# Unread products, one moved gate product and a GpSimd broadcast in a four-layer decoder

## The chip, the cores and the metric

The kernel runs on one core of one Trainium2 chip. The metric is the device time of one execution in microseconds (us); a comparison takes the median of several executions. Besides those, one execution was taken with the hardware profiler, and all rows below come from it.

## The reference

Eight sequences of 56 tokens with 256 channels go through four decoder layers in 32-bit floats. Each layer has three blocks with a residual and a LayerNorm behind each:

```
x = _layernorm(x + attention(x))        # self-attention, another kind in each layer
x = _layernorm(x + cross(x, ctx_512))   # attention over a context of 1500 positions of 64 channels
x = _layernorm(x + experts(x))          # router, top-k, gated experts and a shared expert
```

In layers 0, 2 and 3 the cross-attention has 16 heads, folds the key weights into the query, takes a softmax over the 1500 positions, and multiplies the weights with the rotated context. In layer 1 it attends, under a causal mask, over the first 56 positions of the context. The feed-forward blocks compute `silu(x @ gate) * (x @ up)`, weight it with the router's top-k scores, and multiply with `down`. Only the final `x` is written.

## The kernel before, in words

The program is one sequence of twelve stages (three for each layer). Each stage gives every engine its own list of instructions; nothing schedules them, the order is the one in which the code is written, and engines wait for one another by semaphores with constants (`wait_ge`). A stage's `begin` waits for the normalised `x_feat` (features by tokens) that the stage before put into SBUF. Weights come by DMA from SyncE, mostly a stage ahead.

A TensorE product in 32-bit floats shows as two matmul rows in the trace, one for each pass; the listings of the program's order show it as one. The eight PSUM banks are shared out by number.

- `keep_busy(c, bank, n, rhs, cols)` (L164 to L170) issues `n` products of 128 by `cols` into a bank that nothing reads. It stands at many places in the kernel, each ahead of a wait or between short instructions.
- `cross_attention` (L767 and on, layers 0, 2 and 3). For a pair of sequences, 16 heads by 56 tokens make seven blocks of 128 rows, so four pairs make 28 blocks ("i"), each holding both sequences of its pair. Block i goes through `score` (six products of 500 columns, L1035), maxima on VectorE (L1315, L1320), `exp` on ScalarE (L1236), division on VectorE (L1328), `turn` (48 transposes of 64 columns on TensorE, L1122, in three groups of 16), copies out of PSUM (VectorE L1334 for one group, ScalarE L1243 for two), `weigh` (L1135) and a small copy on GpSimd (L908). The loop at the end of the TensorE list does, for each i, `score(i)`, `weigh(i-2)`, `turn(i-1)`. In its first pass (i = 1) there is no `weigh`, and two `keep_busy` calls stand there. The second group of turnings waits for the exponential of block 1's first half, and the third for that of its second half, since they reuse those banks.
- `feed_forward` (L1429 and on, all layers). TensorE first multiplies `x` with the router (L1483), then for chunk after chunk of 128 hidden columns with `gate` and `up` (`gate_up`, L1501: two products each). VectorE makes the top-k weights from the router's logits; TensorE turns them (`widen`, L1516), VectorE copies them (`wide_out`, L1712), GpSimd spreads one row over all partitions for each chunk (L1474, `partition_broadcast`), VectorE multiplies (L1637), and TensorE does the second product of the chunk (`down`, L361).
- `SmallHeads.tensor` (L1809 and on; layer 1's self- and cross-attention and layer 2's self-attention). Between the scores of the first and of the second group of heads, TensorE waits for VectorE to empty the banks (L1914), with a `keep_busy` ahead of the wait: two products where there is no mask, which is layer 1's self-attention alone.
- `l3_attention` (L2490 and on). Low-rank updates are folded into the weights: TensorE makes the update (`lora`, L2556, L2560), VectorE adds it to the weight (L2720). After the first two updates stands a `keep_busy` of 256 columns, then the first full round of updates, then the values (L1965).

## Time and profile before

| | us |
|---|---|
| three executions | 1661.98, 1663.19, 1670.23 (median 1663.19) |
| the profiled execution, its own time | 1660.22 |
| its span, first to last instruction | 1658.4 |
| TensorE busy in the span | 1620.9 (98%) |
| VectorE / ScalarE / GpSimd busy | 1114.3 / 750.3 / 240.8 |

The span is what the rows below lie in; 1.8 us lie outside it. The granted clock of TensorE is given as a share of 2.4 GHz: 1.00 is that, 0.50 is 1.2 GHz. Its mean over the span is 0.997.

### The profile page before, as it was taken

To read this page: it belongs to the slowest core of one execution; us is meant where nothing else is said; L and a number is where in the kernel's file an instruction comes from. 1 tells how busy PE (TensorE), PEld (TensorE's weight loads), DVE (VectorE), ACT (ScalarE), POOL (GpSimd) and SP (SyncE) were. 2 spreads that over 40 slices of the span, in tenths; PEclk is the share of its full clock that TensorE was granted. 3 is DMA by queue.
4 is the path that set the end of the run, shared out by engine and by line. 5 is a ranking of instruction groups with operands and counts; after the bars stand their busy time and mean duration, and the time that the engine had idled before them with its cause. 6 is when DMAs were issued, how large, how long until landed. Compare 5 with 4: busy or idle time off the path is not lost.

```text
span 1658.4 us, 35648 instructions
## 1 busy us (share of the span) xinstructions
PE 1620.9 (98%) x15234; PEld 1100.1 (66%) x15234; DVE 1114.3 (67%) x1974; ACT 750.3 (45%) x1297; POOL 240.8 (15%) x431
## 2 busy tenths in 40 slices
PE   9999999999999999999999999999999999999998
PEld 5575367777755666655377777764566767777765
DVE  2725889999566763266899999535445289999633
ACT  2223366666412641143366666312454366666411
POOL 0011300000011312011200000010465000000030
PEclk9999999999999999999999999999999999999999
DMA  9312020000040011051020000060300220000010
GB/s 281 84 16 83 1 78 2 2 2 2 2 188 1 2 59 40 1 127 55 1 97 2 2 2 2 2 243 0 64 1 1 115 90 2 2 2 2 2 45 11
DMA packets 35523, 71.10 MB, mean 43 GB/s; under 512 B 25359, under 2 KB 29776, under 8 KB 31434
## 3 DMA queue, kind: packets, MB, share of 16 engines
q1 hardware_dynamic: 35240, 68.71, 12.7%
q8 instruction: 121, 1.98, 0.5%
q14 instruction: 36, 0.29, 0.1%
q10 hardware_dynamic: 126, 0.11, 0.0%
HBM read 68.36 MB, written 0.46 MB: 41 GB/s over the span
## 4 chain that ended last, share of the span: by engine, by line
PE 90%; DVE 6%; ACT 2%; issue 1%; DMA 1%; POOL 0%; DVEq 0%; ACTq 0%; POOLq 0%
PE ps L1122 14%; PE ps L1135 14%; PE ps L1035 13%; PE ps L361 9%; PE ps L1501 9%; PE ps L946 3%; PE ps L2603 3%; PE ps L1150 3%; PE ps L528 2%; PE ps L1965 2%; PE ps L956 1%; PE ps L2630 1%; PE ps L982 1%; PE ps L967 1%; PE ps L523 1%
## 5 line engine op out<-in xcount | busy, mean ns | idle before, releaser
L1236 ACT ACTIVATE arena<-ps,softmax_stats 128x1500 f32<-128x1500 f32 x168 | 254.0, 1512 | 194.0 <-DVE softmax_stats L1317 192.0
L1135 PEld LDWEIGHTS ps<-arena,ctx_pos 125*64 125x64 f32 x4608 | 222.3, 137 | 58.4 <-issue 56.1
L1122 PE MATMUL ps<-ident,arena 64*125 64x64 f32 x4032 | 239.5, 271 | 1.9 <-ACT arena L1236 1.6
L1135 PE MATMUL ps<-arena,ctx_pos 125*64 125x128 f32 (+1 forms) x4608 | 240.5, 262 | 0.0
L1122 PEld LDWEIGHTS ps<-ident,arena 64*125 64x125 f32 x4032 | 227.1, 186 | 17.0 <-issue 13.5
L1035 PE MATMUL ps<-ctx_feat,arena 64*128 64x500 f32 x1008 | 231.7, 592 | 0.0
L1243 ACT COPY arena<-ps 125x512 f32<-125x512 f32 x336 | 172.5, 599 | 78.2 <-PE ps L1122 78.2
L1315 DVE TENSOR_REDUCE softmax_stats<-ps 128x1 f32<-128x500 f32 x252 | 170.7, 679 | 50.4 <-PE ps L1035 50.1
L361 PE MATMUL ps<-arena 128*128 128x256 f32 x736 | 174.9, 384 | 4.9 <-DVE arena L1630 1.2
L1328 DVE TENSOR_SCALAR arena<-arena,softmax_stats 128x1500 f32<-128x1500 f32 x168 | 168.3, 1002 | 5.9
L1501 PE MATMUL ps<-x_feat,arena 128*128 128x448 f32 (+1 forms) x416 | 164.6, 540 | 1.2 <-DVE arena L1613 1.2
L361 PEld LDWEIGHTS ps<-arena 128*128 128x128 f32 x736 | 136.9, 190 | 43.0 <-issue 16.6
L908 POOL COPY arena<-arena 64x128 f32<-64x128 f32 (+1 forms) x186 | 51.5, 277 | 683.7 <-DVE arena L1341 677.6
L1320 DVE TENSOR_REDUCE softmax_stats<-ps 128x1 f32<-128x1500 f32 x84 | 143.6, 1709 | 0.0
L1035 PEld LDWEIGHTS ps<-ctx_feat,arena 64*128 64x128 f32 x1008 | 90.0, 189 | 80.5 <-issue 77.9
L1501 PEld LDWEIGHTS ps<-x_feat,arena 128*128 128x128 f32 (+1 forms) x416 | 78.0, 190 | 63.6 <-issue 59.6
L1334 DVE COPY arena<-ps 125x512 f32<-125x512 f32 x168 | 107.6, 682 | 12.8 <-PE ps L1122 12.5
L1577 ACT ACTIVATE arena<-ps 128x448 f32<-128x448 f32 (+1 forms) x52 | 28.3, 544 | 188.3 <-PE ps L1501 183.9
L1613 DVE TENSOR_TENSOR arena<-ps,arena 128x448 f32<-128x448 f32 x41 | 25.6, 624 | 113.7 <-ACT arena L1577 86.0
L946 PE MATMUL ps<-x_feat,arena 128*128 128x448 f32 x128 | 56.1, 563 | 0.2
L2603 PE MATMUL ps<-x_feat,arena 128*128 128x448 f32 x128 | 52.4, 552 | 1.2 <-issue 0.7
L2731 DVE TENSOR_TENSOR arena<-ps,arena 128x448 f32<-128x448 f32 x32 | 20.0, 625 | 46.0 <-ACT arena L2675 45.9
(325 smaller groups left out, 1923.7 us busy)
## 6 DMA issues: line engine op xcount, KB each, us to landing
ctx_pos<-in_ctx SPq DMA_DIRECT2D x1, 2688.0 KB
arena<-in_L1f_gate SPq DMA_DIRECT2D x1, 2304.0 KB, 11.9
arena<-in_L1f_up SPq DMA_DIRECT2D x1, 2304.0 KB, 16.9
arena<-in_L1f_down SPq DMA_DIRECT2D x1, 2304.0 KB, 7.7
arena<-in_L0a_Wq SPq DMA_DIRECT2D x1, 2048.0 KB, 10.9
arena<-in_L0a_Wc SPq DMA_DIRECT2D x1, 2048.0 KB, 18.8
arena<-in_L0x_Wq SPq DMA_DIRECT2D x1, 2048.0 KB, 10.1
arena<-in_L0x_Wo SPq DMA_DIRECT2D x1, 2048.0 KB, 8.5
```

The source lines that it names most:

```text
L361: m = c.nc.tensor.matmul(y_of(c, s, j), lhsT, rhs, start=False, stop=last, skip_group_check=True)
L946: m = nc.tensor.matmul(c.ps[:, 2 + h % 2, 0:NT], wq[:, k, h, :], c.x_feat[:, k, :, 0:T], start=(k == 0), stop=(k == KT - 1))
L1035: m = nc.tensor.matmul(sc[e][:, k, :], q[e * 64:(e + 1) * 64], c.ctx_feat[e * 64:(e + 1) * 64, j, k * 4 * LP:(k + 1) * 4 * LP], start=True ...
L1122: m = nc.tensor.transpose(c.ps[0:LP, turn_bank(i, k, r), n * 64:(n + 1) * 64], probs[i % 2][e][rows, l * LP:(l + 1) * LP], c.ident[rows, r ...
L1135: m = nc.tensor.matmul(y[r * 64:(r + 1) * 64, lo:hi], c.ctx_pos[:, j, l, e, :], pT[i % 2][:, lo // 64:hi // 64, LT * e + l, :], start=(l = ...
L1236: nc.scalar.activation(probs[i % 2][e].rearrange("p (k l) -> p k l", k=3), sc[e], ACT.Exp, bias=low[:, i % 4, e:e + 1], accum_out=total[:, ...
L1243: nc.scalar.copy(pT[i % 2][:, r, 8 * k:8 * k + 8, :], c.ps[0:LP, turn_bank(i, k, r), :].rearrange("p (s q) -> p s q", s=8)).then_inc(*a_in ...
L1315: nc.vector.tensor_reduce(peak[:, i % 4, k:k + 1], sc[0][:, k, :], AX.X, ALU.max).then_inc(*maxed.next())
L1320: nc.vector.tensor_reduce(low[:, i % 4, 1:2], sc[1], AX.XY, ALU.max, negate=True).then_inc(*lowered[1].next())
L1328: nc.vector.tensor_scalar(probs[i % 2][e], probs[i % 2][e], inv[:, i % 4, e:e + 1], None, ALU.mult).then_inc(*normed[e].next())
L1334: nc.vector.tensor_copy(pT[i % 2][:, r, 0:8, :], c.ps[0:LP, turn_bank(i, 0, r), :].rearrange("p (s q) -> p s q", s=8)).then_inc(*d_in.next())
L1501: m = nc.tensor.matmul(c.ps[0:m_, bank(n) + i, 0:NT], w[:, k, n * 128:n * 128 + m_], c.x_feat[:, k, :, 0:T], start=(k == 0), stop=(k == KT ...
```

## The change

1. In `cross_attention`, the `keep_busy` of 512 columns in the pass i = 1 issues two products instead of one (layers 0, 2 and 3).
2. In `SmallHeads.tensor`, the `keep_busy` without a mask issues four products instead of two (layer 1's self-attention).
3. In `l3_attention`, the `keep_busy` behind the first two updates has 512 columns instead of 256.
4. In `feed_forward` of layers 2 and 3, the first of the two gate products of chunk 0 is issued ahead of the router's products instead of behind them.
5. At the end of each `cross_attention`, GpSimd spreads four numbers of the identity matrix over all partitions into a new tile `reach`, which nothing reads, and waits until that is done.

```diff
@@ cross_attention, gpsimd @@
         pool.wait_ge(ct_in.handle, ct_in.last())
+        nc.gpsimd.partition_broadcast(c.reach[:], c.ident[0:1, 0:4], channels=128).then_inc(*warmed.next())
+        pool.wait_ge(warmed.handle, warmed.last())
@@ cross_attention, tensor, loop over i @@
                 pe.wait_ge(cm_act.handle, cm_act.at(3))
-                keep_busy(c, 6, 1)
+                keep_busy(c, 6, 2)
                 keep_busy(c, 6, 1, None, 256)
@@ feed_forward, tensor @@
         pe.wait_ge(c.loaded[name].handle, 16 * c.expect[name])
+        gate_first = kind in ("L2", "L3")
+
+        def gate_of_first(k):
+            m_ = f.chunks[0][0]
+            nc.tensor.matmul(c.ps[0:m_, bank(0), 0:NT], wg[:, k, 0:m_], c.x_feat[:, k, :, 0:T], start=(k == 0), stop=(k == KT - 1))
+
+        if gate_first:
+            gate_of_first(0)
         for j in range(J):
...
             for i, w in enumerate((wg, wu)):
                 for k in range(KT):
+                    if gate_first and (n, i, k) == (0, 0, 0):
+                        continue
@@ SmallHeads.tensor @@
             if g == 1:
-                keep_busy(c, 6, 2 if self.mask is None else self.waiting)
+                keep_busy(c, 6, 4 if self.mask is None else self.waiting)
@@ l3_attention, tensor @@
-        keep_busy(c, 6, 1, None, 256)
+        keep_busy(c, 6, 1)
```

TensorE in the cross-attention of layer 0, from the last fold of the output weights (L937) over the scores of blocks 0 and 1 to the first turnings, before and then now (line numbers are of each kernel's own file):

```order
L937 MATMUL ps<-arena 64x256 x8
L1035 MATMUL ps<-ctx_feat,arena 128x500 x6
L170 MATMUL ps<-ctx_feat,ident 128x512
L170 MATMUL ps<-ctx_feat,ident 128x256
L1122 MATMUL ps<-ident,arena 125x64 x48
```

```order
L940 MATMUL ps<-arena 64x256 x8
L1038 MATMUL ps<-ctx_feat,arena 128x500 x6
L171 MATMUL ps<-ctx_feat,ident 128x512 x2
L171 MATMUL ps<-ctx_feat,ident 128x256
L1125 MATMUL ps<-ident,arena 125x64 x48
```

One more product of 512 columns stands ahead of the 48 turnings; the same holds in layers 2 and 3.

TensorE at the start of layer 2's feed-forward, from the last filler of the cross-attention to the first `down`; the products of 9 columns are the router, the turnings of 128x128 the widening:

```order
L170 MATMUL ps<-ctx_feat,ident 128x256
L314 MATMUL ps<-ident,x_tok 128x128 x2
L186 MATMUL ps<-x_tok,ident 128x256
L1477 UNCONDITIONAL_BRANCH
L1483 MATMUL ps<-arena,x_feat 128x9 x8
L1501 MATMUL ps<-x_feat,arena 128x448 x8
L1516 MATMUL ps<-ident,arena 128x128 x8
L1501 MATMUL ps<-x_feat,arena 128x448 x4
L361 MATMUL ps<-arena 128x256 x4
```

```order
L171 MATMUL ps<-ctx_feat,ident 128x256
L315 MATMUL ps<-ident,x_tok 128x128 x2
L187 MATMUL ps<-x_tok,ident 128x256
L1480 UNCONDITIONAL_BRANCH
L1488 MATMUL ps<-x_feat,arena 128x448
L1494 MATMUL ps<-arena,x_feat 128x9 x8
L1514 MATMUL ps<-x_feat,arena 128x448 x7
L1529 MATMUL ps<-ident,arena 128x128 x8
L1514 MATMUL ps<-x_feat,arena 128x448 x4
L362 MATMUL ps<-arena 128x256 x4
```

One gate product went ahead of the router, and the seven others of chunks 0 and 1 stayed behind it; the number of products is the same.

GpSimd from the last copies of layer 2's cross-attention to the broadcasts of its feed-forward:

```order
L908 COPY arena<-arena 64x64 x4
L908 COPY arena<-arena 64x128 x4
L1457 UNCONDITIONAL_BRANCH
L1461 MEMSET arena 128x8x8 x2
L1462 MEMSET arena 128x1536
L1463 MEMSET arena 128x4x8
L1474 ISA
L1474 ISA arena<-arena 128x448 x10
```

```order
L909 COPY arena<-arena 64x64 x4
L909 COPY arena<-arena 64x128 x4
L911 ISA
L911 ISA reach<-ident 128x4
L1460 UNCONDITIONAL_BRANCH
L1464 MEMSET arena 128x8x8 x2
L1465 MEMSET arena 128x1536
L1466 MEMSET arena 128x4x8
L1477 ISA arena<-arena 128x448 x10
```

The library change (the `ISA` row without operands) went with the new broadcast from the feed-forward to the end of the cross-attention. Layers 0 and 3 show the same.

## Rows read from the trace of the kernel before

**Rows 1.** The page: each engine's busy us, its share of the span, instructions.

```profile
PE 1620.9 (98%) x15234; PEld 1100.1 (66%) x15234; DVE 1114.3 (67%) x1974; ACT 750.3 (45%) x1297; POOL 240.8 (15%) x431
```

**Rows 2.** Windows: length, each engine's busy us, granted clock, DMA share, GB/s.

```profile
79.00:82.40 3.40, 3.40 (x26) 2.12 (x24) 1.77 (x3) 0.54 (x1) 0.70 (x1) 0.50 1.03 333
215.50:218.90 3.40, 2.77 (x43) 2.42 (x42) 3.32 (x5) 2.80 (x4) 0.00 (x0) 1.00 1.03 431
218.90:222.35 3.45, 3.45 (x20) 1.97 (x18) 2.01 (x4) 2.05 (x4) 0.00 (x0) 0.51 0.97 394
834.06:837.46 3.40, 2.77 (x43) 2.42 (x42) 3.32 (x5) 2.80 (x4) 0.00 (x0) 1.00 0.97 404
837.46:840.91 3.45, 3.45 (x28) 1.53 (x26) 2.79 (x6) 2.05 (x4) 0.00 (x0) 1.00 1.01 427
```

**Rows 3.** Timeline of TensorE: start, us, operation, [idle before, releaser]; layers 0 and 2.

```profile
218.38 1.43 PE L1122 MATMUL ps<-ident,arena 64*125 64x64 f32 x16 [0.54 <-ACT arena L1236]
219.60 4.12 PE L1035 MATMUL ps<-ctx_feat,arena 64*128 64x500 f32 x12
...
834.14 2.26 PE L1122 MATMUL ps<-ident,arena 64*125 64x64 f32 x32
836.94 1.08 PE L1122 MATMUL ps<-ident,arena 64*125 64x64 f32 x16 [0.54 <-ACT arena L1236]
837.86 2.92 PE L1035 MATMUL ps<-ctx_feat,arena 64*128 64x500 f32 x12
...
843.48 2.83 PE L1122 MATMUL ps<-ident,arena 64*125 64x64 f32 x48
```

**Rows 4.** Timeline of VectorE, layer 2's cross-attention, first turnings.

```profile
836.43 1.29 DVE L1334 COPY arena<-ps 125x512 f32<-125x512 f32 x2
837.83 1.00 DVE L1328 TENSOR_SCALAR arena<-arena,softmax_stats 128x1500 f32<-128x1500 f32 x1
840.82 0.68 DVE L1315 TENSOR_REDUCE softmax_stats<-ps 128x1 f32<-128x500 f32 x1 [0.34 <-PE ps L1035]
```

**Rows 5.** The chain that ended last, layer 2's feed-forward: start, us, what.

```profile
1085.01 0.64 DVE arena L1712
...
1085.69 2.05 issue
1087.73 0.75 POOL arena L1474
```

**Rows 6.** Timeline: TensorE's wait in layer 2's feed-forward, and GpSimd around library changes.

```profile
1089.48 1.99 PE L361 MATMUL ps<-arena 128*128 128x256 f32 x8 [1.06 <-DVE arena L1637]
...
1056.25 0.64 POOL L908 COPY arena<-arena 64x128 f32<-64x128 f32 x2 [7.49 <-DVE arena L1341]
1076.48 0.23 POOL L1461 MEMSET arena<- 128x64 f32 x2 [19.58 <-DVE x_feat L265]
1087.73 5.03 POOL L1474 PARTITION_BROADCAST arena<-arena  x7 [9.64 <-issue]
...
1592.78 1.36 POOL L1474 PARTITION_BROADCAST arena<-arena  x2 [8.29 <-DVE arena L1712]
```

**Rows 7.** Timeline of TensorE, layer 1's self-attention, between two groups of scores.

```profile
542.00 1.88 PE L170 MATMUL ps<-ctx_feat,ident 128*128 128x512 f32 x4
545.73 1.12 PE L1827 MATMUL ps<-arena 32*64 32x112 f32 x64 [1.85 <-DVE arena L1914]
```

**Rows 8.** The chain that ended last, start of layer 3's self-attention.

```profile
1135.24 0.63 PE ps L170 x2
1135.88 0.43 PE ps L2556
```

**Rows 9.** Timeline, layer 2's feed-forward: first gate and up products, router's weights, first widening.

```profile
1078.28 6.26 PE L1501 MATMUL ps<-x_feat,arena 128*128 128x448 f32 x16
1083.28 0.22 DVE L1698 TENSOR_TENSOR arena<-arena 128x32 f32<-128x32 f32 x1
1084.37 1.04 PE L1516 MATMUL ps<-ident,arena 128*128 128x128 f32 x8
```

More of the change, by code:

```diff
@@ L69, in __init__ @@
         self.warm = sb("warm", [128, 1])
+        self.reach = sb("reach", [128, 4])
         self.std = sb("std", [128, J])
@@ L820, in cross_attention @@
         s.sem(x) for x in ("maxed", "turned_lo", "turned_hi", "d_in", "a_in", "pv_mm", "kept", "ct_in", "ct_last"))
-    cm_mm, padded = s.sem("cm_mm"), s.sem("padded")
+    cm_mm, padded, warmed = s.sem("cm_mm"), s.sem("padded"), s.sem("warmed")
     cm_act, cm_dve = s.sem("cm_act"), s.sem("cm_dve")
```

## The prediction, written before the changed kernel ran

> **What bounds the kernel now.** I read the page first. TensorE is busy for 1620.9 of 1658.4 us [rows 1], so only 37.5 us of its time are idle, and an edit that takes no product away can win no more than some waits and whatever time TensorE spends at its lower clock. The change takes no product away. I then read the granted clock over the span in windows. It falls to 1.2 GHz in two places: for 3.45 us in layer 0's cross-attention (0.51), and for 3.40 us in layer 0's self-attention (0.50), which the change leaves alone [rows 2]. Last I read the timeline and the chain that ended last at each of the edited places.
>
> **The low clock and the extra filler in the cross-attentions.** Layers 0 and 2 run the same instructions there, so one is the price list of the other. In both, the 3.40 us around the first turnings have TensorE busy for 2.77 us with 43 matmuls. In layer 0 the clock then fell to 0.51; in layer 2 it stayed at 1.00 [rows 2]. The low stretch costs this: from the start of the third group of turnings to the end of the next scores, layer 0 takes 219.60 + 4.12 - 218.38 = 5.34 us and layer 2 takes 837.86 + 2.92 - 836.94 = 3.84 us [rows 3]. TensorE is on the path in both, so a low stretch here is worth 1.50 us.
>
> The Trainium skill (TensorE: Matmul & The Clock Gate, "What's actually happening") says that the gate watches activity on its own beat, which does not restart with the kernel. By it two equal stretches may end differently, and this trace agrees: 2.77 us busy in both, 0.51 behind one and 1.00 behind the other [rows 2]. By that rule an unchanged kernel gets another number of low stretches in each execution; this is the second rival below.
>
> The new product of 512 columns is issued three times (layers 0, 2, 3). Two such products take 1.88 us in layer 1 [rows 7], so one takes 0.94. What covers it is TensorE's own idle time ahead of the third group of turnings, which waits for ScalarE's second exponential (0.54 us in both layers [rows 3]). The least cover is the 0.63 us that TensorE is idle in the stretch (3.40 - 2.77 [rows 2]). The most follows from the unhindered rate of turnings, 48 in 2.83 us: 32 of them need 1.89, and from 834.14 to 836.94 there are 2.80, which leaves 0.91 [rows 3]. So each filler puts 0.03 to 0.31 us on the path. I take 0.10, near the end that comes from back-to-back turnings, since those behind the filler no longer wait for the first exponential: 0.30 us for the three. The second group of turnings gets later by about half a microsecond, and with it VectorE's copies of it (836.43), the division (837.83) and the next block's maxima; VectorE still waits 0.34 us for TensorE before 840.82 [rows 4], and ahead of that for two more scores, so I put nothing on that.
>
> **The broadcast at the end of the cross-attentions.** In layer 2's feed-forward the chain runs through 2.05 us of "issue" on GpSimd between VectorE's copy of the widened weights, which ends at 1085.65, and the first broadcast at 1087.73 [rows 5]. Nothing that the profile shows holds GpSimd there; it has been without a busy instruction for 9.64 us since its memsets [rows 6]. The only thing between them is the library change. In layer 3 there were 8.29 us between, and what released the broadcast was VectorE's copy [rows 6]. So I read the change of library as lasting 8 us or less there, and 9.6 us where layer 3's weights were arriving at the same time. Moved behind the last copy of the cross-attention, which ends at 1056.89, it begins 19.6 us ahead of the next memset at 1076.48 [rows 6]. 9.64 for the library and 0.75 for a broadcast, taken as long as one of 448 columns [rows 5], are 10.4; the new wait holds up only those memsets, and has 9.2 us to spare. Layers 0 and 3 have the same gap. VectorE and TensorE do not wait for this broadcast.
>
> TensorE waited 1.06 us for the first weighted tile [rows 6]. The broadcast can move forward by up to 2.05 us, and then TensorE is last, with the products of the third chunk. The gain is 1.06 us, bounded by 0 (the delay stays) and 2.05 (all of the gap).
>
> The Trainium skill (GPSIMD Engine Reference, "2.1 Instruction dispatch") says that the first call into freshly loaded code costs about 6 us, seen as a gap behind the configuring instruction with no row of its own. The gap without a row agrees, the size does not: 9.64 us here [rows 6]. With 6 us the library would have been ready at about 1084, ahead of the data, and this part would give nothing; the sum below would then come out 1.06 us higher.
>
> **The gate product ahead of the router (layers 2 and 3).** It is moved, not added. A product is two of the 16 rows that take 6.26 us, so 0.78 us [rows 9], and the router's logits come that much later. Behind them VectorE's work on the weights ended at 1083.50, and TensorE began to widen them at 1084.37, when it was through with its products [rows 9]: 0.87 us of slack against 0.78. Bounds are 0 and 0.78 for each layer; I take 0.10 each, since TensorE fetches the weights of a turning a little before it begins: 0.20 us. Neither layer shows a low clock here, so nothing comes back.
>
> **The filler in layer 1's self-attention.** Two more products of 512 columns are 1.88 us, against 1.85 us that TensorE waits for VectorE right behind them [rows 7]. I take 0.05, with bounds 0 and 1.88.
>
> **The filler in layer 3's self-attention.** Here the chain runs through the filler itself: 0.63 us for 256 columns, and the next update right behind it [rows 8]. No wait covers it, so twice the columns cost more: at least 0.94 - 0.63 = 0.31, at most 0.63 again. Half of 0.94 is 0.47, which I take.
>
> **Sum against the profiled execution.** -1.50 (low stretch of layer 0) - 1.06 (broadcast) + 0.30 + 0.20 + 0.05 + 0.47 = -1.54 us. From 1660.22 that is 1658.7. The median of the three runs is 1663.19, which is 2.97 us above the profiled execution: as much as two more low stretches at 1.50. If they lie elsewhere, the change gives 1663.19 - 1.54 = 1661.65; if one of them lies at an edited place and goes too, 1660.15. I say 1661.0, between the two, nearly 0.13% below the median. A measurement of this kernel can tell 0.5% from no change, 8.3 us, so this is "no change" by that bound.
>
> **Rivals.**
> - *The low stretches only move.* If filler does not decide where the clock falls, the median keeps its low stretches and the change is -1.06 + 1.02 = -0.04: 1663.15. For it: the equal stretches with unequal ends [rows 2]. Against it: TensorE's idle time in the stretch that preceded the fall is filled.
> - *The library was not what delayed the broadcast.* Then the 1.06 us stay: 1661.0 + 1.06 = 1662.1. Against it: nothing else stands between the memsets and the broadcast.
> - *The fillers meet a low clock and stand on the path.* TensorE takes its instructions in order, so a filler at 1.2 GHz pushes everything behind it. At half the clock one takes 1.88 us: 3 x (1.88 - 0.63) + (3.76 - 1.85) + 0.94 = 6.6 us, less 1.06 for the broadcast, +5.5: 1668.7, slower than before. It decides as soon as the clock has already fallen when the filler starts. Against it: the clock was at 1.00 when the turnings behind the present filler began, in layer 0 too [rows 2], and the full price needs the fall at every place; one place costs 0.9 to 1.9 us.
>
> **How the numbers follow.** Forecast 0.62, stretches only move 0.20, library not the cause 0.08, fillers on the path 0.10. For the range the low end is 1656.5: the profiled execution with this change is 1658.7, and less the low stretch of layer 0's self-attention, 1.50, is 1657.2, with the rest of the broadcast's bound below that. The high end is 1666.5: half of the third rival's extra, and the three runs of before reach 1670.23, so a median can sit a few us high. For faster by over 0.5% it would have to fall below 1654.9, which no sum of the gains from the fastest execution reaches: 0.03. For slower by over 0.5% it would have to pass 1671.5, above even the third rival: 0.03. That leaves 0.94.
>
> **What would show each step.** In the profile after: GpSimd's first broadcast in layer 2's feed-forward 0.2 to 0.3 us behind the copy of the widened weights, and no wait for VectorE ahead of the first `down` of that stage; the granted clock at 1.00 through the first turnings of all three cross-attentions, with the idle time ahead of the third group at 0.1 or less; layer 1's wait of 1.85 us gone, with the next scores at the same distance from VectorE's subtraction; the update rounds of layer 3 some 0.45 us later against the first two updates; the first widening of layers 2 and 3 at most 0.2 us later against the start of its stage. The prediction is wrong if the wait for the first tile stays, if a low stretch follows the fillers, or if the median leaves 1656.5 to 1666.5.

## The result, and the profile after

The changed kernel took 1656.45 us (median of 8 runs, 1655.58 to 1664.71) against 1664.80 for the kernel before in the same comparison (8 runs, 1661.98 to 1674.96). The ratio is 0.9949, with a 95% interval from 0.9924 to 0.9973: faster by 8.35 us or 0.5%. I had forecast 1661.0 and a range from 1656.5; the time lies 0.05 us below that range. Of the gain I had forecast a quarter (2.2 us below 1663.19), and I had called it "no change". By the prediction's own bound of 0.5% it is just over, with the interval on both sides of that bound; that it is not zero is clear. The profiled execution of after took 1655.68 us, with a span of 1653.9 and a mean granted clock of 0.999.

In the windows of the profile after (columns as in [rows 2]), the first two rows are layer 0's cross-attention around the first turnings, the third layer 2's, the fourth layer 3's, the fifth layer 0's self-attention. They answer to [rows 2]:

```profile
212.00:215.42 3.42, 3.42 (x22) 1.86 (x22) 3.15 (x6) 2.12 (x3) 0.00 (x0) 1.00 0.86 293
215.42:218.84 3.42, 3.42 (x46) 2.64 (x44) 2.88 (x5) 2.25 (x5) 0.00 (x0) 1.00 1.02 427
834.20:837.60 3.40, 3.40 (x26) 1.54 (x26) 3.12 (x7) 2.05 (x4) 0.00 (x0) 1.00 1.01 428
1342.00:1345.40 3.40, 3.40 (x50) 2.66 (x50) 3.11 (x5) 1.79 (x2) 0.00 (x0) 1.00 0.88 375
78.00:81.40 3.40, 3.05 (x37) 2.08 (x35) 1.80 (x4) 1.37 (x3) 0.94 (x1) 1.00 1.00 361
```

Both stretches at 1.2 GHz that the prediction reads in the profile before are gone. That of layer 0's self-attention, in the last row, went although the change does nothing there. (In both profiles the clock falls once more in the last 2 to 3 us of the span, from 1656.0 before and 1651.2 after, behind TensorE's last product; that is left out of all counts here.) The same place in the timeline of TensorE after (start, us, operation; compare [rows 3]) has no wait ahead of the third group of turnings any more:

```profile
212.27 2.42 PE L171 MATMUL ps<-ctx_feat,ident 128*128 128x512 f32 x6
214.62 3.02 PE L1125 MATMUL ps<-ident,arena 64*125 64x64 f32 x48
217.48 2.92 PE L1038 MATMUL ps<-ctx_feat,arena 64*128 64x500 f32 x12
```

GpSimd after, from the end of layer 2's cross-attention into its feed-forward, answers to [rows 6]:

```profile
1059.39 0.28 POOL L911 PARTITION_BROADCAST reach<-ident  x1 [5.81 <-issue]
1073.16 0.24 POOL L1464 MEMSET arena<- 128x64 f32 x2 [13.49 <-DVE x_feat L266]
1073.33 1.38 POOL L1465 MEMSET arena<- 128x1536 f32 x1
1074.65 0.12 POOL L1466 MEMSET arena<- 128x32 f32 x1
1082.49 2.28 POOL L1477 PARTITION_BROADCAST arena<-arena  x3 [7.72 <-DVE arena L1725]
```

The library change now stands ahead of `reach` (5.81 us), and the large broadcast is released by VectorE. TensorE in the same stage, in the timeline, has its first gate product ahead of the router, and no wait ahead of the first `down` (1.06 us before [rows 6]):

```profile
1073.15 1.02 PE L1488 MATMUL ps<-x_feat,arena 128*128 128x448 f32 x2
1074.01 1.85 PE L1494 MATMUL ps<-arena,x_feat 128*128 128x9 f32 x16
1075.71 5.51 PE L1514 MATMUL ps<-x_feat,arena 128*128 128x448 f32 x14
1081.06 1.04 PE L1529 MATMUL ps<-ident,arena 128*128 128x128 f32 x8
1081.93 3.17 PE L1514 MATMUL ps<-x_feat,arena 128*128 128x448 f32 x8
1084.94 1.89 PE L362 MATMUL ps<-arena 128*128 128x256 f32 x8
```

The stage starts 3.32 us earlier than before (the memset at 1073.16 against 1076.48 [rows 6]). The timelines of TensorE, set side by side product for product, say where that comes from. Before:

```profile
8.72 12.27 PE L528 MATMUL ps<-x_feat,arena 128*128 128x448 f32 x32
...
82.69 1.05 PE L563 MATMUL ps<-arena 128*128 128x2 f32 x8
...
223.65 2.84 PE L1135 MATMUL ps<-arena,ctx_pos 125*64 125x128 f32 x48
...
829.93 2.79 PE L1035 MATMUL ps<-ctx_feat,arena 64*128 64x500 f32 x12
...
840.71 2.84 PE L1135 MATMUL ps<-arena,ctx_pos 125*64 125x128 f32 x48
```

After:

```profile
8.06 12.27 PE L529 MATMUL ps<-x_feat,arena 128*128 128x448 f32 x32
...
80.87 1.05 PE L564 MATMUL ps<-arena 128*128 128x2 f32 x8 [0.35 <-DVE arena L706]
...
220.33 2.84 PE L1138 MATMUL ps<-arena,ctx_pos 125*64 125x128 f32 x48
...
826.63 2.79 PE L1038 MATMUL ps<-ctx_feat,arena 64*128 64x500 f32 x12
...
837.40 2.84 PE L1138 MATMUL ps<-arena,ctx_pos 125*64 125x128 f32 x48
```

The changed kernel is 0.66 us ahead 8 us into the span, before anything that was edited; 1.82 behind the first low stretch of before, in layer 0's self-attention (1.16 more); and 3.32 behind the second, at layer 0's first turnings (1.50 more). From there to layer 2's feed-forward nothing is gained or lost. So 1.82 of the 3.32 us came at places that the change does not touch. The last place is the chain that ended last at the start of layer 3's self-attention (start, us, what), where [rows 8] had 0.63 us for the filler:

```profile
1128.62 1.98 PE ps L2569 x4
1130.60 1.06 PE ps L171 x2
1131.65 0.43 PE ps L2569
```

Layer 3 begins 4.65 us earlier (TensorE's first update at 1128.62 against 1133.27), so 1.33 us came in layer 2's feed-forward; the filler took 0.43 of that, and 0.31 came back in the middle of layer 3's self-attention, for a reason that no run shows. Together that is the 4.54 us between the two profiles (1660.22 to 1655.68). The medians differ by nearly twice as much. The mean granted clock of each run says where the rest is: over 113 runs of the kernel before it has a median of 0.993, over 14 runs of the changed kernel 0.9985. The profiled run of before, at 0.997, was one with little low clock: 13 of the 113 had as high a one. At the same granted clock the two kernels lie close together: at 0.998, 7 runs of before have a median of 1658.42 us and 3 of the changed kernel 1657.22; at 0.997, 6 have 1660.24 and 3 have 1658.66. So all but 1.2 to 1.6 us of the gain goes with the clock.

### The profile page after: what moved, and what is told of

It reads as the page before. It is cut to its first block, busy times and chain, and to the rows that moved or that the text cites. A ratio compares the mean times of both kernels' runs of the same rounds, so it can differ in the third digit from the quotient of the medians.

```text
span 1653.9 us, 35671 instructions
## 1 busy us (share of the span) xinstructions
PE 1621.0 (98%) x15244; PEld 1100.4 (67%) x15244; DVE 1113.4 (67%) x1974; ACT 749.7 (45%) x1297; POOL 240.9 (15%) x434
## 4 chain that ended last, share of the span: by engine, by line
PE 91%; DVE 5%; ACT 2%; issue 1%; DMA 1%; POOL 0%; DVEq 0%; ACTq 0%; POOLq 0%
PE ps L1125 14%; PE ps L1138 14%; PE ps L1038 13%; PE ps L362 9%; PE ps L1514 9%; PE ps L949 3%; PE ps L2616 3%; PE ps L1153 3%; PE ps L529 2%; PE ps L1978 2%; PE ps L959 1%; PE ps L171 1%; PE ps L2643 1%; PE ps L985 1%; PE ps L970 1%
```

## The experiments

Theory: an ordinary execution of before has several stretches at half clock, not two, most of them at the edited places, and the change takes them out. Rival: they fall anywhere, and the profile's two went by luck. Four kernels first, each the changed one with one part taken back.

**The cross-attentions' product taken back.**

```diff
-                keep_busy(c, 6, 2)
+                keep_busy(c, 6, 1)
```

> The changed kernel with one unread product instead of two ahead of the first turning in the three cross-attentions; all else as changed. Base: the changed kernel, 1655.6 us with no stretch at half clock, median 1656.45; a half-clock stretch cost 1.50 us in the profile of before; two more products cost about 0.10 us at each of three places. Theory A (the low-clock stretches of an ordinary execution sit mostly at the first turnings of the three cross-attentions, where the trace of before has PE waits of 0.54 us): median about 1660.0 (three stretches at 1.50 come back, 0.30 goes), mean granted clock about 0.997 down from 0.999. Rival B (only the one stretch that the profile showed in L0's cross-attention hangs on them): 1656.6 to 1657.5. Rival C (the stretches fall wherever the chip's phase puts them and not on these waits): 1656.2, within 0.3 of the changed kernel.

1660.87 us (12 runs, 1656.32 to 1668.83), 4.4 above the changed kernel: theory A. Its profile, of a run in the lower group (1658.83), has a stretch at half clock in layer 0's cross-attention again, for 3.4 us from 218.6, and none in those of layers 2 and 3. The runs fall in two groups, six up to 1658.83 and six from 1662.91 up.

**Layer 1's products taken back** (four to two).

```diff
-                keep_busy(c, 6, 4 if self.mask is None else self.waiting)
+                keep_busy(c, 6, 2 if self.mask is None else self.waiting)
```

> The changed kernel with two unread products instead of four in L1's self-attention, where PE waited 1.85 us for VectorE in the profile of before; all else as changed. Theory A: the wait there is part of a long busy stretch and holds no stretch at half clock: 1656.4, within 0.4 of the changed kernel. Rival B (this wait of 1.85 us is the longest at an edited place, and most of the five stretches that a median execution of before had over the changed one begin at it or behind it): 1659 to 1662, two to four stretches at 1.50 us. Rival C (one stretch in most executions): 1657.5 to 1658.

1657.22 (1655.43 to 1667.28, three over 1662.5), fastest run as with the change. In the timeline of this kernel the wait of 1.85 us is back, and the clock stays at 1.00 around it, as theory A has it. The median is 0.8 above the changed kernel's where A allowed 0.4; that is within what these runs scatter.

**The gate product put back behind the routers.**

```diff
-        gate_first = kind in ("L2", "L3")
+        gate_first = False
```

> The changed kernel with the first gate product no longer ahead of the routers in the FFNs of L2 and L3; all else as changed. Its direct price is 0 us by the trace after (8.07 us from the first product to the widening in L2, as before). Theory A: without it 1656.4, within 0.4 of the changed kernel. Rival B (the products of one weight tile behind the routers stood behind a thin stretch in which the clock fell in some executions, in L2 or L3): one or two stretches come back, 1657.5 to 1659.5. Rival C (it takes the place of work that would have stood beside a weight transfer and costs now): 1655.5 or less.

1657.87 (1655.49 to 1658.95), 1.4 above: rival B, and its profile has a stretch at half clock right behind layer 2's router, from 1076.7 on. I had put nothing there. The fastest runs are alike (1655.49 and 1655.58), so it is the low stretch that costs, not the order: at full clock the widening begins 7.90 us behind the stage's first product before and 7.91 after, and not 8.07 as the expectation says.

**Layer 3's product back at 256 columns.**

```diff
-        keep_busy(c, 6, 1)
+        keep_busy(c, 6, 1, None, 256)
```

> The changed kernel with the product at the end of L3's self-attention back at 256 columns instead of 512; all else as changed. Its direct price in the profile after was 0.43 us (1.06 against 0.63 on the chain of waits), with nothing beside it. Theory A (it is only a price): 1656.0, that is 0.4 below the changed kernel, at the same clock of 0.999. Rival B (its columns keep a stretch at half clock away in the short span between L2's FFN and L3's attention): one stretch of 1.50 us comes back in most executions, 1657.5. Rival C (two or more come back): 1659 or more.

1658.16 (1654.97 to 1666.66). The fastest run is 0.6 below the changed kernel's, as a price of 0.43 would have it; the median is 1.7 above. Inconclusive alone.

Then three parts of the change alone in the kernel before, and the changed kernel without its broadcast. The first, the cross-attentions:

```diff
-                keep_busy(c, 6, 1)
+                keep_busy(c, 6, 2)
```

> The kernel before with one part of the change alone: two unread products ahead of the first turning in the three cross-attentions. So far: runs fall in two groups about 8 us apart, one of 1655 to 1659 and one of 1663 to 1669; 1 of 8 runs of the changed kernel lies in the upper one, 6 of 12 with this part taken out, 0 to 3 of 12 with another part taken out, and before has 24 of 35 at or above 1662.9 (its own floor stands 1.06 + 0.27 us higher, for the broadcast). Theory A (the cross-attentions' products are what takes runs out of the upper group): median 1658 to 1660, at most 3 of 12 runs over 1662.9. Rival B (it takes several parts together): median 1661.5 to 1663, about half of the runs over 1662.9. Rival C (this part takes out only the one stretch of 1.50 us in L0): median about 1663, 1.5 below before.

1661.53 (1658.70 to 1668.14; ratio to before 0.9970, 0.9945 to 0.9995). Five of 12 runs over 1662.9 and a gain of 5.4 against 1666.90 in the same comparison: rival B, by the median and by the count.

Layer 1's products alone:

```diff
-                keep_busy(c, 6, 2 if self.mask is None else self.waiting)
+                keep_busy(c, 6, 4 if self.mask is None else self.waiting)
```

> The kernel before with one part of the change alone: four unread products instead of two in L1's self-attention, where PE waited 1.85 us for VectorE. Theory A (the upper group hangs on the cross-attentions): same as before, median 1664 to 1665, two runs in three over 1662.9. Rival B (every part thins out the upper group a little): median about 1662 to 1663. Rival C (this wait alone brings the clock down): median 1659 to 1660. If its profile falls into the upper group, it shows where the 8 us lie: as five stretches of about 3.4 us at half clock, either in one place in a row or in several attention stages.

1664.01 (ratio 1.0001, 0.9971 to 1.0031): theory A. No effect of this part on the time can be seen. Its profile (1663.98) has five stretches at half clock, in layer 0's self-attention, layer 2's cross-attention and feed-forward, layer 3's self-attention and layer 3's feed-forward.

The gate product alone (with the lines of the change that issue and skip it):

```diff
+        gate_first = kind in ("L2", "L3")
```

> The kernel before with one part of the change alone: the first gate product ahead of the routers in the FFNs of L2 and L3. Taking this part out of the changed kernel left 1657.87 (12 runs from 1655.49 to 1658.95, none in the upper group) against 1656.45. Theory A (upper group from the cross-attentions alone): median 1664 to 1665 as before. Rival B (the gate product takes one stretch of 1.50 us out): 1663. Rival C (it brings the upper group about in some runs, as its absence had none there): 1665 or more.

1662.62 (1659.55 to 1671.53; ratio 0.9981, 0.9953 to 1.0009): nearest to rival B, though the interval does not shut out no effect. Its profile took 1669.68 us and shows what the upper group holds. In the windows of this kernel, at the head of layer 3's cross-attention:

```profile
1301.00:1304.40 3.40, 2.44 (x19) 2.07 (x18) 0.00 (x0) 0.37 (x1) 0.00 (x0) 1.00 1.03 423
1304.60:1308.00 3.40, 3.40 (x14) 2.69 (x13) 0.00 (x0) 0.00 (x0) 0.00 (x0) 0.51 0.99 425
...
1318.20:1321.60 3.40, 3.40 (x6) 1.68 (x5) 0.00 (x0) 1.36 (x4) 0.00 (x0) 0.50 0.00 0
1321.80:1325.20 3.40, 3.40 (x30) 3.17 (x28) 0.00 (x0) 1.73 (x5) 0.00 (x0) 1.00 0.01 2
```

TensorE is busy for 2.44 of 3.40 us while it waits for the weight Wq, then the clock stays at half for 17 us and comes back. The price shows in the timelines of TensorE, of this kernel and of before, from the filler behind that wait to the next products that are at full clock in both:

```profile
1304.19 1.67 PE L171 MATMUL ps<-ctx_feat,ident 128*128 128x512 f32 x2 [0.96 <-DMA arena<-in_L3x_Wq]
...
1316.63 5.75 PE L1018 MATMUL ps<-x_feat,arena 128*128 128x448 f32 x8
1322.22 1.90 PE L994 MATMUL ps<-arena 96*128 96x64 f32 x16
```

```profile
1304.50 1.12 PE L170 MATMUL ps<-ctx_feat,ident 128*128 128x512 f32 x2 [0.82 <-DMA arena<-in_L3x_Wq]
...
1314.26 1.90 PE L993 MATMUL ps<-arena 96*128 96x64 f32 x16
```

1322.22 - 1304.19 = 18.03 us against 9.76: one such stretch costs 8.27 us, about the distance of the two groups. Most of the products in it have 64 columns, but it lasts into a round of four with 448 (L1018).

**The changed kernel without the broadcast at the end of the cross-attentions.**

```diff
-        nc.gpsimd.partition_broadcast(c.reach[:], c.ident[0:1, 0:4], channels=128).then_inc(*warmed.next())
-        pool.wait_ge(warmed.handle, warmed.last())
```

> The changed kernel without the small broadcast at the end of each cross-attention, so that the large one in each FFN is the first of its kind after other GpSimd work again. Base: the changed kernel, 1656.45 with 1 run of 8 in the upper group. Theory A (in L2's FFN the chain of waits went through the broadcast, 9.64 us with a wait of 0.75 us on POOL, and 1.33 us went there in the trace after): lower group's fastest runs at 1656.6 to 1656.9, 1.06 to 1.33 above the 1655.58 of the changed kernel; median 1657.5 to 1659. Rival B (the transfers of L2's weights set the stage, not the broadcast): fastest 1655.6, no difference. Rival C (it costs in L3's and L0's FFN too, where the trace of before has it off the chain): fastest 1658 or more.

1659.85, fastest 1658.43. The timeline of its GpSimd and TensorE (two views, in this order) in layer 2's feed-forward:

```profile
1084.26 5.02 POOL L1475 PARTITION_BROADCAST arena<-arena  x7 [9.54 <-issue]
```

```profile
1086.01 1.35 PE L362 MATMUL ps<-arena 128*128 128x256 f32 x5 [0.96 <-DVE arena L1648]
```

The stage begins 0.05 us earlier than in the profile after, and TensorE begins layer 3's self-attention at 1129.80 instead of 1128.62: 1.23 us for the broadcast, theory A in the price. By the time it is rival C, whose fastest run is 1658 or more, but C's reason is not there: in the feed-forwards of layers 0 and 3 VectorE releases the first large broadcast with the part in and without it. The fastest run is 2.8 above; a stretch at half clock stands at the start of layer 3's self-attention in this profile (1132.0 on), with the clock at 0.998 in its six fastest runs. Whether the late broadcast brings that about, and with it the other 1.6 us, was not tried by itself.

Next the two parts together in the kernel before, a filler at the long stretch, a version with more fillers, and the changed kernel again.

The two parts together:

```diff
-                keep_busy(c, 6, 1)
+                keep_busy(c, 6, 2)
...
+        gate_first = kind in ("L2", "L3")
```

> The kernel before with two parts of the change: two products ahead of the first turnings of the three cross-attentions, and the first gate product ahead of the routers of L2 and L3. The profiles so far show stretches of 3.4 us at half clock at the first turnings in 4 of 12 places without the cross products and in 0 of 18 with them, and behind the routers of L2 and L3 in 4 of 8 without the moved gate product and in 0 of 12 with it. Theory A (these two parts are the whole of the clock's share, and the broadcast and the 256 columns the rest): fastest run 1656.5 (the changed kernel's 1655.6 plus 1.33 less 0.43), median 1657.5 to 1659, 0 to 3 of 12 runs in the upper group. Rival B (the other parts are needed for the upper group): median 1660 to 1662, five or more runs over 1663. Rival C (the means of the two parts alone simply add, 3.6 and 2.3 us below before): mean 1660.3.

1660.88 (9 runs, 1657.41 to 1667.11; ratio 0.9959, 0.9941 to 0.9977), 5.8 below before: rival B in the median, but one run over 1663 where B has five; the mean of 1660.7 is near rival C's 1660.3. Three runs sit at 1657.4 to 1657.8 and five at 1660.5 to 1661.9. Its profile (1667.11) has the long stretch in layer 3, 17 us from 1303.5, and none at an edited place.

The kernel before with a filler at the head of layer 3's cross-attention:

```diff
                 if t == 2:
+                    keep_busy(c, 5, 2)
                     arrived("_next")
```

> The kernel before with two unread products of 512 columns more at one place that the change does not touch: in the first part of L3's cross-attention, ahead of the wait for its weight Wq (0.82 us idle in the trace of before), bank 5. The one profile that fell into the upper group has 17.06 us at half clock there from 1304.5 on, through the products of 64 columns that follow. Direct price about 0.15 us. Theory A (the upper group is this stretch, and the wait starts it): no run over 1667, spread from 1658 to 1666, median 1661 to 1662.5. Rival B (upper runs are many single stretches in other places): as before, median 1664.8 to 1666.9, a third of the runs over 1667.5. Rival C (the stretch is there, but it hangs on the 64-column products behind the wait, not on the wait): as B in time, and the profile shows it at the same place.

1663.99 (1659.95 to 1667.63; ratio 0.9982, 0.9966 to 0.9998). No run passes 1667.63, where 9 of 20 runs of before in the same comparison do, and 47 of all 113. That suggests that the long stretch is a good part of before's upper tail; no profile of the kernel before itself shows one. The median is 2.7 us below that of before, short of theory A's 1661 to 1662.5: the filler lengthens TensorE's list by 0.68 us, and the runs hold many single stretches, as rival B has it. The profile of this kernel (1667.47) has seven, and no long one. Its windows, in order: layer 0's self-attention, layer 2's first turnings, layer 2's router, the start and the middle of layer 3's self-attention, layer 3's first turnings, layer 3's router:

```profile
78.40:81.80 3.40, 3.40 (x30) 2.72 (x28) 1.17 (x3) 0.54 (x1) 0.94 (x1) 0.51 1.01 365
836.00:839.40 3.40, 3.40 (x16) 1.73 (x14) 1.79 (x4) 2.05 (x4) 0.00 (x0) 0.51 1.02 434
1078.30:1081.70 3.40, 3.40 (x6) 1.44 (x6) 1.64 (x16) 1.69 (x3) 0.00 (x0) 0.52 0.97 305
1136.30:1139.70 3.40, 3.40 (x16) 1.33 (x11) 2.45 (x5) 0.00 (x0) 0.00 (x0) 0.52 0.00 0
1283.40:1286.80 3.40, 3.40 (x22) 2.83 (x23) 1.83 (x6) 0.69 (x2) 0.00 (x0) 0.53 0.02 5
1348.20:1351.60 3.40, 3.40 (x20) 2.36 (x22) 1.65 (x4) 1.90 (x4) 0.00 (x0) 0.52 1.00 426
1590.60:1594.00 3.40, 3.40 (x8) 1.89 (x8) 1.07 (x9) 1.51 (x2) 0.00 (x0) 0.53 0.90 371
```

The changed kernel with that filler and two edits more:

```diff
+            if g == 0:
+                keep_busy(c, 2, 1)
             pe.wait_ge(diag_in.handle, diag_in.at(g + 1))
...
-        keep_busy(c, 6, 1)
+        keep_busy(c, 6, 1, None, 256)
```

> The changed kernel with L3's self-attention product back at 256 columns (0.43 us less), the two products more in L3's cross-attention ahead of its wait for Wq, and one product of 512 columns ahead of the wait of 0.68 us for GpSimd in the first round of L0's self-attention, where three of ten profiles have a stretch at half clock around 78 to 82 us that no part of the change touches. Theory A (all three hold): fastest 1655.2 to 1655.4, median 1655.6 to 1656.3, no run in the upper group. Rival B (L0's product only moves its stretch, L3's does not stop the long one): as the changed kernel, 1656.4, one to three runs of 12 over 1663. Rival C (the products lengthen the path by up to 1 us): fastest 1656.0 or more.

1656.87 (6 runs, 1656.18 to 1657.12): rival C for the fastest run, theory A for the upper group. In the timelines the new products lengthen TensorE's list by 0.30 us in layer 0 and 0.67 in layer 3. No run left 1657.2, so it is the steadiest version, but not faster.

The changed kernel, without an edit:

> The changed kernel, unaltered, beside the others on one chip. So far 8 runs, median 1656.45, one in the upper group. Theory A (its upper group has the same share as in the kernels with one part other than the cross-attentions' taken out, 9 of 48): 1 to 4 of 12 runs over 1663, median 1656.3 to 1657.5. Rival B (all parts together take it out): none over 1659, median 1656.0. Rival C (no different from the kernel without the cross-attentions' products): six of 12 over 1663, median about 1660.

1656.44 (6 runs, 1655.51 to 1658.94): rival B by the count, for none is over 1659, but not by the median, which is in theory A's range. With the first 8 that makes 14 runs, median 1656.45, one over 1659.

Last, both parts taken out of the changed kernel, the two small parts taken out, and smaller fillers.

```diff
-                keep_busy(c, 6, 2)
+                keep_busy(c, 6, 1)
...
-        gate_first = kind in ("L2", "L3")
+        gate_first = False
```

> The changed kernel with both the cross-attentions' second product and the moved gate product taken out; what is left of the change is the broadcast, L1's and L3's products. Before and changed kernel: 1664.8 to 1666.9 and 1656.45. Theory A (those two parts carry the clock's share, some 6 to 8 us, and the rest is 1.23 for the broadcast less 0.43): median 1663 to 1665.5, fastest 1656.5 to 1658, a mean granted clock near 0.994. Rival B (any one part left in keeps most stretches away): 1660 to 1661, as with the cross-attentions' products alone taken out (1660.87). Rival C (the broadcast, too, keeps stretches away, as the kernel without it had 0.998 in its best runs): 1661 to 1662.5.

1662.81 (1658.77 to 1665.11), 6.4 above the changed kernel: between theory A and rival C. Its profile (1661.95, 6.27 us over that of the changed kernel) has four stretches, all four at places of these two parts. Windows of this kernel, layer 0's first turnings, layer 2's router, layer 3's first turnings and router, and, at full clock, layer 2's first turnings:

```profile
216.60:220.00 3.40, 3.40 (x22) 2.41 (x22) 1.64 (x3) 1.74 (x4) 0.00 (x0) 0.51 0.98 405
1076.90:1080.30 3.40, 3.40 (x6) 1.59 (x5) 1.69 (x17) 1.69 (x3) 0.00 (x0) 0.53 0.92 328
1342.90:1346.30 3.40, 3.40 (x18) 1.92 (x18) 1.96 (x4) 2.05 (x4) 0.00 (x0) 0.51 1.04 443
1585.20:1588.60 3.40, 3.40 (x6) 1.68 (x7) 1.48 (x15) 1.51 (x2) 0.00 (x0) 0.51 0.97 409
834.00:837.40 3.40, 2.86 (x32) 1.83 (x30) 3.24 (x6) 2.23 (x5) 0.00 (x0) 1.00 1.00 425
```

The first four are full of work and at half clock; ahead of each stands a piece with a wait or with the router's narrow products. The price can be read behind layer 2's router: in this kernel's timeline of TensorE

```profile
1074.49 1.95 PE L1494 MATMUL ps<-arena,x_feat 128*128 128x9 f32 x16
...
1084.09 1.04 PE L1529 MATMUL ps<-ident,arena 128*128 128x128 f32 x8
```

the widening begins 9.60 us behind the stage's first product; in the profile after it is 1081.06 - 1073.15 = 7.91: 1.69 us. Read in the same way against the profile after, the others cost 1.52 (layer 0's turnings), 1.50 (layer 3's turnings) and 1.69 us (layer 3's router).

The two small parts out:

```diff
-                keep_busy(c, 6, 4 if self.mask is None else self.waiting)
+                keep_busy(c, 6, 2 if self.mask is None else self.waiting)
...
-        keep_busy(c, 6, 1)
+        keep_busy(c, 6, 1, None, 256)
```

> The changed kernel without L1's two products more and with L3's at 256 columns, so that the cross-attentions' products, the moved gate product and the broadcast are left. Theory A (L1's part does nothing, and L3's costs 0.43 us and keeps no stretch away): fastest 1655.0, median 1656.0 to 1657.5. Rival B (L3's or L1's product keeps one or two stretches away, which would explain 1660.88 for the two parts alone without the broadcast): fastest 1655.0, but median 1658 to 1660. Rival C (both cost only): 1655.5 and none over 1657.

1657.63 (1655.97 to 1668.45), four runs over 1662.5: nearest to theory A by the median (A to 1657.5, B from 1658), but the fastest run is 1.0 above the 1655.0 that A and B have, and the median is 1.2 above the changed kernel's. Its interval (0.9942 to 0.9987 of before) overlaps that of the changed kernel in the second comparison (0.9916 to 0.9955). Whether layer 3's product keeps anything away stays open.

The version with smaller fillers:

```diff
+                    keep_busy(c, 5, 1)
                     arrived("_next")
...
+            if g == 0:
+                keep_busy(c, 2, 1, None, 256)
             pe.wait_ge(diag_in.handle, diag_in.at(g + 1))
...
-        keep_busy(c, 6, 1)
+        keep_busy(c, 6, 1, None, 256)
```

> The changed kernel with L3's self-attention product at 256 columns, one product of 512 columns ahead of the wait for L3's Wq (idle 0.63 to 0.84 us there in the traces so far), and one of 256 columns ahead of the wait of 0.67 us for GpSimd in L0's self-attention. In the version with two and with 512 columns they cost 0.67 and 0.30 us and no run of 6 went over 1657.2. Theory A (the smaller ones fit into the waits and do the same): fastest 1655.1 to 1655.4, median 1655.5 to 1656.2, none over 1660. Rival B (they fit, but keep nothing away): fastest 1655.1, median 1656 to 1657.5, one or two of 12 over 1660. Rival C (they still cost): fastest 1655.8 or more.

1656.33 (6 runs, 1655.50 to 1662.57; 0.9936 of before, 0.9911 to 0.9962). Not to be told from the changed kernel: nearest to rival B, with one run of six over 1660. The profile has one stretch, at layer 3's first updates. No version beats the changed kernel by more than the scatter.

**All profiles together.** Seventeen profiles (before, after and these) say more than one comparison, since each place either has a stretch at half clock or not:

| place | the part not in | the part in |
|---|---|---|
| first turnings of the three cross-attentions | 8 of 18 | 0 of 33 |
| behind the routers of layers 2 and 3 | 8 of 12 | 0 of 22 |
| the wait in layer 1's self-attention | 0 of 7 | 0 of 10 |
| layer 3's first updates | 3 of 10 | 1 of 7 |
| layer 0's self-attention (not edited) | 7 of 15 | |
| head of layer 3's cross-attention (not edited) | 3 of 14, two of them 17 us long | |
| layer 0's first products, at 8 us (not edited) | 3 of 17 | |
| middle of layer 3's self-attention (not edited) | 2 of 17 | |
| behind layer 1's router (not edited) | 0 of 17 | |

The rows for layer 0's self-attention and for the head of layer 3's cross-attention leave out the kernels that have a filler there (0 of 2 and 0 of 3).

## Why the prediction was wrong

- **The count of low stretches: the step that failed.** I took the 2.97 us between the profile and the median of three runs for two more stretches and let "one of them at most" sit at an edited place. An ordinary execution of before holds about five more than the changed kernel: 8.35 us, less 1.23 - 0.43 = 0.80 for the rest, are 7.5 us, at 1.50 each. The granted clocks say the same by another way: 0.993 over a span of 1663.8 us is 23 us at half clock (2 x 0.007 x 1663.8), 0.9985 over 1654.6 is 5, and the 18 us between them are five stretches of 3.4. By the table the edited places hold 3 x 8/18 + 2 x 8/12 = 2.7 of them in a mean execution; up to four showed at once. I had the evidence of a range: 1661.98 to 1670.23 is 8 us for one kernel, and the last of these runs is 10 us from the profile, six or seven times 1.50.
- **"Neither layer shows a low clock here, so nothing comes back"** (the gate product) fell with it. That was read from one execution. Behind the router the clock was low in 8 of 12 cases without the move and in none of 22 with it. I priced this part at +0.20; it costs 0.01 us in the profile after (7.91 against 7.90), and taking it out costs 1.4 us by the medians.
- **The cross-attentions' fillers** did in layer 0 what was said, and the same in layers 2 and 3, where the profile before showed no low clock. Their own price, 0.10 each, is not seen: in layer 2, at full clock in both profiles, the first scores to the first `weigh` take 840.71 - 829.93 = 10.78 us before and 837.40 - 826.63 = 10.77 after. That the profile before showed the fall in layer 0 and not in the two others looks like chance: in the kernels without the part it stands in 3, 2 and 3 of 6 profiles of layers 0, 2 and 3.
- **The price of a stretch**, 1.50 us, held: 1.52 and 1.50 at first turnings, 1.69 behind a router, in the kernel with both parts out. The long stretch, 8.27 us, had no term.
- **The broadcast**: forecast -1.06. TensorE's wait of 1.06 is gone, and taking the part out costs 1.23 us of the stage. The mechanism held. The library itself took less than the 9.64 us, or "8 us or less", that I read: 5.81 us ahead of `reach`.
- **Layer 3's filler**: forecast +0.47, measured 1.06 - 0.63 = 0.43. **Layer 1's**: forecast +0.05. VectorE's row ended at 545.60 before, 0.13 us ahead of the scores [rows 7], and at 542.26 after, 0.15 ahead: nothing either way.
- **The profiled execution** was forecast at 1658.7 and took 1655.68. Of the 3.0 us between, 1.82 came at places that the change does not touch, which is luck. The rest: the new products and the moved one cost 0.43 us and not 1.02, the broadcast gave 1.33 and not 1.06, and 0.31 came back in layer 3.
- **The low end of the range** does not follow from its own terms: 1657.2 less the rest of the broadcast's bound, 2.05 - 1.06, is 1656.2, and I wrote 1656.5. The measured time lies between the two, and a range from 1656.2 would have had the count of stretches just as wrong.
- **The rivals.** That the stretches only move, which stands first in the list and not second as the text ahead of it says, fell: none appears at the first turnings or behind the routers with the part in. At layer 3's first updates one of 7 does. That the fillers stand on the path at half clock fell. The rival that was missing was that the kernel before has more to lose than its profile shows.

Not settled: how the whole gain splits. That nearly all of it is the clock is shown by the runs' granted clocks. The table's 2.7 stretches at 1.50 to 1.69 us and 0.80 make 4.9 to 5.4 of 8.35 us. The two parts tried together say more: 6.4 us when both are taken out of the changed kernel, 5.8 when they stand alone in the kernel before; with 0.80 that is 6.6 to 7.2. The remainder may lie in the upper group, with its long stretch in layer 3: 40 of 113 runs of before pass 1668, and the highest of 14 runs of the changed kernel is 1664.71. The change edits nothing at that place. The changed kernel without the moved gate product had none in 12 runs either, so I can name no part for it; that the earlier stretches shift what comes behind them may decide it, but that was not tried.

## What to carry to other kernels

Read the granted clock of every run beside its time before counting what a profile shows: where a median stands 3 us above the profiled execution and the runs spread by 8, the profile is the exception, and what the others lose sits at thin places that look harmless in it. A thin place (a router of 8 or 9 columns, a first pass that waits half a microsecond) is worth a moved product where the order allows one (0.01 us here), and an unread one where it fits into an existing wait (one of 512 columns cost nothing in layer 2's cross-attention, and 0.30 to 0.68 us went where the new products did not fit). To find out what a filler does, pool many profiles by place; a comparison of medians with two groups of runs 8 us apart cannot tell parts of 1 us.

## What the runs showed of the hardware

The half clock falls on work that is dense: all windows above at 0.50 to 0.53 have TensorE busy for their whole length, and at the edited places what is thin lies just ahead. Narrow products alone do not bring it about: layer 1's router, with 16 columns, takes 1.85 us where the edited ones took 1.95, and no profile has a stretch behind it. It lasted 3.4 us at most places, but 17 us in two profiles, where most of the products behind the wait have 64 columns. It cost 1.50 to 1.69 us at the turnings and routers, 1.16 us in layer 0's self-attention, and 8.27 us when long. In two executions the same places fell: the five stretches of the kernel with layer 1's part alone are all among the seven above, and the first four of them begin within 0.04 us of the same moment of the span. And GpSimd's change of library shows as a gap of 5.74 to 6.11 us ahead of `reach` (30 cases; the DMA share there was 0.00 to 0.01 in the profile after). In layer 2's feed-forward of six of the seven kernels without `reach`, while layer 3's weights came in (DMA share 0.96 before), the gap ahead of the first broadcast was 9.54 to 10.52 us; in the seventh the data came last. That the weights make it longer is not shown by itself.
